# Weights and constants behind the first spreads, their low halves on GpSimd alone, and norm 1 behind the last maxima

## The reference, cut to what matters

```python
x = x + attention(layernorm(x), ctx, ctx, Wq, Wk, Wv, Wo)       # 16 batches of 256 tokens, width 256
x = x + ffn(layernorm(x), gate_w, w1, b1, w2, b2, sw1, sb1, sw2, sb2)
# attention: 16 heads of 16, softmax over pairs of 64-blocks (rows r, cols c, |r - c| <= band)
# ffn: out = shared(x) + sum over 2 experts e of relu(mask_e * x @ w1[e] + b1[e]) @ w2[e] + b2[e],
#      mask_e from the argmax of x @ gate_w.T; shared(x) = relu(x @ sw1 + sb1) @ sw2 + sb2
```

## Time and profile before

| | |
|---|---|
| median of 3 runs | 923.95 us (922.97 to 925.59) |
| the profiled execution, its own time | 924.62 us |
| its span | 922.8 us |
| PE busy | 798.9 us, 87% |
| DVE busy | 612.6 us, 66% |
| ACT busy | 498.0 us, 54% |
| POOL busy | 422.7 us, 46% |
| mean granted TensorE clock | 0.956 |

### The profile page before, as it was taken

One profiled execution on the slowest core, in us unless ns is written; L12 is line 12 of the kernel. 1 busy time (PEld: TensorE's weight loads), 2 busy tenths in 40 slices (PEclk: granted clock), 3 DMA queues, 4 the chain that ended last, 5 costly groups with the idle time before them and its releaser, 6 DMA issues.

```text
span 922.8 us, 24416 instructions
## 1 busy us (share of the span) xinstructions
PE 798.9 (87%) x8374; PEld 665.5 (72%) x8374; DVE 612.6 (66%) x1255; ACT 498.0 (54%) x1150; POOL 422.7 (46%) x773
## 2 busy tenths in 40 slices
PE   2165887879999999999999999999999999989894
PEld 2144756567887878687878787887878687858894
DVE  4558567476767677786858586767678685845231
ACT  2345453546565564757465656556574746465452
POOL 3455332343537373644546363637364554455311
PEclk9568899999999999999999999999999999999998
DMA  6767321263634444445445353434444444414630
GB/s 189 198 185 255 101 77 47 81 197 103 198 94 135 159 120 154 142 137 158 144 129 178 114 193 102 154 123 135 159 124 143 153 139 128 156 47 138 223 122 23
DMA packets 97389, 128.19 MB, mean 139 GB/s; under 512 B 14656, under 2 KB 82624, under 8 KB 97089
## 3 DMA queue, kind: packets, MB, share of 16 engines
q1 hardware_dynamic: 89760, 107.89, 37.9%
q0 software_dynamic: 6624, 18.95, 6.2%
q10 hardware_dynamic: 960, 0.79, 0.4%
HBM read 90.80 MB, written 37.04 MB: 139 GB/s over the span
## 4 chain that ended last, share of the span: by engine, by line
PE 49%; DVE 21%; DMA 13%; issue 6%; ACT 4%; SPq 4%; POOL 1%; DVEq 1%; POOLq 0%; ACTq 0%
PE acc L729 12%; PE nd L643 12%; PE hid L538 10%; DVE nmax L1186 9%; DMA QP<-scratch_m 5%; PE work L627 5%; DMA scratch_m<-mT 3%; PE work L671 2%; DVE xhat L1159 2%; PE work L538 2%; DVE PT L1229 2%; DVE T L1202 1%; PE work L594 1%; DVE check L1197 1%; SPq L341 1%
## 5 line engine op out<-in xcount | busy, mean ns | idle before, releaser
L1469 POOL TENSOR_TENSOR hl<-h,hh 128x256 fp32r<-128x256 f32 x228 | 172.3, 762 | 327.3 <-ACT hh L988 327.1
L972 ACT ACTIVATE PT<-work 128x512 f32<-128x512 f32 x192 | 106.1, 604 | 63.4 <-PE work L627 63.3
L1205 DVE RECIPROCAL T<-nd 128x256 f32<-128x256 f32 x51 | 89.4, 1753 | 42.9 <-PE nd L643 42.8
L729 PE MATMUL acc<-w_hi,hh 128*128 128x256 f32 (+1 forms) x528 | 113.6, 297 | 0.0
L538 PE MATMUL hid<-Xs,W 128*128 128x256 f32 x816 | 110.0, 288 | 0.2
L988 ACT ACTIVATE h<-hid,bias 128x256 f32<-128x256 f32 x144 | 69.1, 480 | 74.1 <-PE hid L538 74.1
L538 PEld LDWEIGHTS hid<-Xs,W 128*128 128x128 f32 x816 | 103.4, 195 | 2.7 <-DVE Xs L1139 0.9
L729 PE MATMUL acc<-w_lo,hh 128*128 128x256 f32 (+1 forms) x528 | 105.1, 281 | 0.0
L538 PE MATMUL hid<-Xr,W 128*128 128x256 f32 x768 | 104.1, 285 | 0.0
L538 PEld LDWEIGHTS hid<-Xr,W 128*128 128x128 f32 x768 | 94.2, 188 | 5.1
L643 PE MATMUL nd<-PT,V 128*32 128x256 f32 x1024 | 84.0, 400 | 10.1 <-DVE T L1202 4.5
(11 more groups left out here) (196 smaller groups left out, 1654.5 us busy)
## 6 DMA issues: line engine op xcount, KB each, us to landing
W<-w1q SPq DMA_DIRECT2D x64, 512.0 KB, 6.0
KP<-scratch_k SPq DMA_DIRECT2D x192, 64.0 KB, 2.4
QP<-scratch_q SPq DMA_DIRECT2D x180, 64.0 KB
scratch_k<-T SPq DMA_DIRECT2D x16, 512.0 KB, 3.5
scratch_q<-T SPq DMA_DIRECT2D x16, 512.0 KB, 3.2
yt<-yq SPq DMA_DIRECT2D x17, 260.0 KB, 2.8
xt<-xq SPq DMA_DIRECT2D x17, 256.0 KB, 3.8
xin<-x SPq DMA_DIRECT2D x16, 256.0 KB, 3.5
```

What stands on the lines that cost most here:

```text
L729: mm = nc.tensor.matmul(acc[:, t, :], R(h[:, u % 2, a, P * t:P * t + P]), R(row), start=first, stop=u == UNITS - 1 and h is hl and a == 1, ...
L972: nc.scalar.activation(PT[:, j % 4].rearrange("p t q -> p (t q)"), score_bank(j), ACT.Exp).then_inc(sem["exp_done"], 1)
L1205: nc.vector.reciprocal(T[:, p, :], nd[:, p % 2, 1, :]).then_inc(sem["inverted"], 1)
L1469: nc.gpsimd.tensor_tensor(R(hl[:, u % 2, a]), h32[:, u % 2, a], hh[:, u % 2, a], ALU.subtract).then_inc(sem["hl_done"], 1)
```

## The change

It has two parts.

In the start and in iteration 0: POOL's weight loads and SP's constants both wait for `q_spread1`, the second half of the spread Q. DVE no longer makes low halves of weights (it made every second one of the first 14); POOL makes all 24. They are handed out over iteration 0 by the table `SPLITS_AT`: 4 ahead of it, 2 and 2 around the projections of the next batch, one for each of the eight head pairs, then 3, and 5 at the very end. The sums of the constants on DVE (`make_constants`) move from ahead of the maxima to behind the Q projection of batch 1, with two temporary homes in `xhat2`, and PE's wait for them moves from `maxima` to the first `scores_t`. SP's first residual load moves behind them.

In all iterations from 1 on: DVE's `norm1_apply` moves from between the third and fourth group of maxima to behind the last; `gate_scores(n, 1)` and `choose` move from behind the second group to behind the third; `move_ids` moves to the head of the division loop; `ranks` on PE moves behind visit 3. On PE, ACT and DVE, K of the next batch stands ahead of `xT`.

```diff
-EARLY_PIECES = 4
-STAGES, BY_VECTOR = 5, 14
+STAGES = 5
+SPLITS_AT = (4, 0, 0, 0, 0, 2, 2, 1, 1, 1, 1, 1, 1, 1, 1, 3, 5)
...
         def slot_pieces(k):
-            return range(EARLY_PIECES + 2 * (k - 1), EARLY_PIECES + 2 * k)
+            return range(sum(SPLITS_AT[:k]), sum(SPLITS_AT[:k + 1]))
...
# SP
-            sp.wait_ge(sem["proj_lo"], 4)
+            sp.wait_ge(sem["q_spread1"], 96)
             for dst, src in ((bias1[:, :], b1), (bsum[:, :], blocksum), (hsum[:, :, :], headsum),
...
-            sp.wait_ge(sem["consts_read"], 1)
-            load_residual(0, first=True)
             iteration(0, False, False, True)
# PE
             def maxima(i):
-                if type(i) is int and i == 0:
-                    pe.wait_ge(sem["consts_read"], 1)
...
                 if p == 0:
                     pe.wait_ge(sem["shift_spread"], 32 * i + 32)
+                    if type(i) is int and i == 0:
+                        pe.wait_ge(sem["consts_read"], 1)
...
                     shared_up(n, 2)
-                    ranks(n, claim(i, ("rk", 0), tile=tile))
                 visit(i, 3, more)
                 if shared:
+                    ranks(n, claim(i, ("rk", 0), tile=tile))
                     shared_down(n, 1)
...
                 if more:
+                    front_project(i + 1, "k", 1, c_hi, c_lo, "c_lo")
                     front_xT(i + 1)
-                    front_project(i + 1, "k", 1, c_hi, c_lo, "c_lo")
# ACT, iteration
                 for p in range(PAIRS):
-                    if p == 2:
-                        splits(i, 7)
-                    if p == 5:
-                        splits(i, 8)
+                    splits(i, 7 + p)
...
-                splits(i, 9)
+                splits(i, 15)
...
-                splits(i, 10)
+                splits(i, 16)
# DVE, iteration
                     for j in range(4 * v, 4 * v + 4):
                         maximum(i, j)
-                        if shared and j == 13:
+                        if shared and j == 14:
                             rank_tokens(n)
-                    splits(i, v + 1)
...
-                    if shared and v == 1:
+                    if shared and v == 2:
                         gate_scores(n, 1)
-                        if type(i) is not int or i > 1:
-                            move_ids(n - 1)
                         choose(n)
-                    if shared and more and v == 2:
-                        norm1_apply(i + 1)
...
+                if shared and more:
+                    norm1_apply(i + 1)
                 low(i, "mT_hi", work[:, BANK[("mT", 0)], 0:P], mT[:, 0, :], mT[:, 1, :], "m_lo")
...
+                if type(i) is int and i == 0:
+                    make_constants()
                 for p in range(PAIRS):
                     if p == 0:
+                        if shared and (type(i) is not int or i > 1):
+                            move_ids(n - 1)
# POOL
-            pool.wait_ge(sem["first_q_bounced"], 16)
+            pool.wait_ge(sem["q_spread1"], 96)
             for n in range(STAGES):
                 load(n)
...
                 if more:
                     context_low(i + 1)
-                for k in range(3 if shared else 5, 10):
+                for k in range(5, 16):
                     splits(i, k)
...
                 reciprocal_deviation(i, 1)
-                splits(i, 10)
+                splits(i, 16)
```

More of the change, by code:

```diff
@@ L225, in loaded @@
             return sem[f"stage_loaded{SLOTS[n]}"], 16 * SLOTS[:n + 1].count(SLOTS[n])
[L227 to L230 removed]
         def low_done(n):
[L234 to L235 removed]
+            return sem["stage_lo"], n + 1
         def slot_pieces(k):
[L239 removed]
+            return range(sum(SPLITS_AT[:k]), sum(SPLITS_AT[:k + 1]))
         def low_half(g, a):
@@ L416, in iteration @@
                     load_x(i + 2)
-                if type(i) is not int or i > 0:
+                if type(i) is int and i == 0:
+                    sp.wait_ge(sem["consts_read"], 1)
+                    load_residual(0, first=True)
+                else:
                     load_residual(i)
```

71 lines of the change are left out of this document (21 added, 50 removed).

## The result

The changed kernel takes 914.65 us (median of 6 runs, 914.43 to 918.78) against 924.6 for the kernel before (6 runs): ratio 0.9907, 95% interval 0.9892 to 0.9921. The prediction was 914.4. The profiled execution spans 912.7 us instead of 922.8.

The account below looks back on a forecast made before the run. PE, busy 87% of the span, was taken as nearly the bound from iteration 4 on. Loop 5.3 us (6.4 + 1.2 - 2.3) plus start 4.3 (8.7 - 1 - 3.4) gave 9.6: 914.4 us, range 907 to 921.

Parts of the forecast that it names:

- the first wait: PE's 0.66 us ahead of visit 3's odd scores: becomes a wait for the mask at ranks, 0.1 comes back.
- the second: PE's 0.71 us wait ahead of the transposition of the maxima: goes, 0.7 gained per iteration.
- a gate score waits for c_lo: DVE, steady loop: one gate score stands until POOL's c_lo ends at 406.3, so the mask is there at 407.1.
- norm 1 is free: DVE, behind the last maxima: norm 1 takes 0.8 with POOL idle and costs nothing; without that cover 0.4.
- my 0.8: Gain per steady iteration, 0.1 + 0.7 from the two waits; over eight iterations 6.4 us.
- the price of the gate's move: Iterations 1 to 4: gate scores of about 1.5 replace a norm of 1.2; losses 0.3, 0.1, 0.5, 0.4.
- Iterations 1 to 4 gain nothing from the norm: Norm 1's move wins nothing there: iteration 4 transposes without a wait, in 1 to 3 maxima are late for other reasons.
- that chain: Start: from POOL's c_lo at 41.4 through K, xT, Q and constant sums, 10.1 us; transposed scores at 51.5, 8.7 earlier.
- The tail: End of iteration 0: five POOL splits behind norm 2's deviation delay visit 1 of iteration 1; 3.4 us lost, at least 2.7.
- nothing blocks the gate scores: Rival, steady loop: gate scores meet no POOL instruction; loop gains 12.4, start 4.3, 907.3 us; chance 0.13.
- The late pieces behind the store: Rival, iteration 1: last pieces land late, PE waits 8 us, start gives nothing back; 918.7 us; chance 0.17.
- The rival in which the mask holds PE longer in every iteration: At ranks behind visit 3: mask at 408.3, PE goes on 1.1 later; 930.6 us; chance 0.07.

Follow-up runs that it names:

- experiment 2: The changed kernel with the order of the loop put back as before, only the new start kept: 921.4 us, ratio 0.9963.
- experiment 10: The changed kernel with xT ahead of K again in all engines: 913.1 us, ratio 0.9864.
- Experiment 3: The changed kernel with gate scores, mask and ranks at their old places, norm 1 still behind the last maxima: 910.3 us, ratio 0.9857.
- experiment 5: The changed kernel with the store to w1q held until all 24 weight pieces have their low halves: 913.9 us, ratio 0.9871.
- experiment 4: The changed kernel with POOL making c_lo behind the third hidden unit's low halves from iteration 1 on: 907.1 us, ratio 0.9809.
- experiments 5 to 10: The changed kernel with store later (913.9 us), even splits (917.7), both (915.5), context first (913.3), constants first as well (913.0), or xT first (913.1).
- 6: The changed kernel with two of the five last weight pieces made inside iteration 0's division loop: 917.7 us, ratio 0.9900.
- 8: The changed kernel with the context of batch 1 split ahead of the first four weight pieces: 913.3 us, ratio 0.9862.
- experiment 9: The changed kernel with batch 1's context split ahead of the first four weight pieces and constant sums ahead of Q's low half: 913.0 us, ratio 0.9874.
- experiment 12: The changed kernel with later c_lo, gate scores, mask and ranks at old places in iterations 1 to 3, and context and constants first: 894.5 us, ratio 0.9674.

## Why the prediction was right, and where it was not

**The steady loop.** Predicted 7.6 from iteration 5 on (6.4 + 1.2), measured 8.3. The steps are as described: the first wait changes its name, the second goes, a gate score waits for c_lo, norm 1 is free. The eight iterations with both waits gained 1.03 each on average, 8.3 in all for 6.4, and iteration 15 gained 1.0 for 0.6. Against that, iteration 5 lost 1.2 where I had a gain of 0.3 (50.3 for 49.1). PE waits in iteration 4's division loop, between the two transpositions, which the kernel before did not do:

```profile
275.86 0.64 PE L638 MATMUL nd<-PT,V 128*32 128x256 f32 x8 [1.19 <-DVE T L1197]
```

DVE is late there because it waits 5.07 for the DMA of `scratch_q`, 3.54 before. A wait at this place (0.54 to 1.33) stands in all experiments but 2, so it comes with the new loop; why that DMA ends later is open. The 0.2 that each of the eight gained beyond my 0.8 is as large as a wait that I had not counted (0.21 to 0.45 for `scratch_m` ahead of the transposed scores before, at most 0.20 after). But with xT first (experiment 10) waits of up to 0.48 are back there and the iterations are not longer for it, so the cause of the 0.2 is not shown.

**Iterations 1 to 4.** Predicted -2.3, measured -0.8 in the profiled execution, but by other terms. What failed is the price of the gate's move: 1.3 (0.3, 0.1, 0.5 and 0.4 in iterations 1 to 4). Experiment 3 measures 5.0 for it, of which 3.9 are idle time of PE: the mask alone is waited for 0.32, 1.12, 1.11 and 1.31. In iteration 4, where I had 0.4, DVE is held by two instructions of POOL and not one. "Iterations 1 to 4 gain nothing from the norm" is off as well, by an amount that is not settled. With norm 1 (and K) moved and the gate left, they take 165.7 instead of 169.9. PE's idle time is 24.6 for 25.7 there, so of the 4.2 only 1.1 is waiting, and the rest is busy time, 141.1 for 144.2, at a granted clock of 0.97 for 0.94. Busy time differs by 3.4 between the kernel before and experiment 2, which have the same loop. The two errors nearly cancel; that is luck.

**The start.** Predicted 4.3, measured 2.6. The transposed scores came at 52.4 for 51.5. The two waits in that chain, 1.50 for a_lo and 2.43 for the constant sums, were in my sum (1.4, and 1.3 + 1.1); the 0.9 is many small sizes: K starts 0.4 later than I had it, Q 0.2 later behind K, and the scores 0.3 later behind Q. The division loop lost 1.9 and not 1 (21.2 before, 23.1 now), at the upper end of its 0 to 2. The tail cost 3.4 as predicted (11.2 to 14.55 from attention's output to visit 1), for the reason given, POOL's five splits; the late loads beside the store lay under it, as experiment 5 shows. Also, this execution was 0.8 ahead of that of before at 15 us, where the kernels don't yet differ, so the start's own gain is nearer 2. The runs give the start alone 3.4 (1.9 to 4.8).

**The sum** hit, 914.4 for 914.65, partly by luck: it was 0.7 too low from iteration 5 on, 1.5 too low in iterations 1 to 4 and 1.7 too high in the start. The steps named for the start and the steady iterations are what the traces show, and the sizes are off by up to 2 us in each part.

**The rivals.** That nothing blocks the gate scores was worth 907.3 by the prediction; made true, it is 907.1, though from iteration 5 on it gained 18.0 where that price had 12.4, and in the profiled execution the start and iterations 1 to 4 together lost 0.7 (91.6 and 171.6) where it had a gain of 4.3; the agreement is in part chance. The late pieces behind the store happened and were covered. The rival in which the mask holds PE longer in every iteration did not come: in iterations 5 to 14 the wait is 0.61 to 0.71. But what it described, a gate score and then the mask held by two instructions of POOL, is what iteration 4 shows, with a wait of 1.31. Where c_lo was moved onto the mask, in iterations 2 and 3 of experiment 4, the wait is 2.05 and 2.04.

**What stays open.** Why iterations 1 to 4 take 171 us in the changed kernel and 174 to 178 in experiments 5 to 10, whose order is the same there but for xT and K in one. It is mostly busy time at a lower clock (142.2 us busy in the changed kernel, 144.9 to 149.5 in these). Each was profiled once, and the runs of one kernel among them differ by up to 6.7 us; in 5, 6, 8 and 10 the profiled execution was the slowest of its kernel, in 9 the fastest. That a late gate costs 3 to 4 us of waiting in iterations 1 to 4 is shown by the idle times. That it also costs clock is argued: experiment 9 has half clock behind the mask's waits of iterations 2 and 3, the changed kernel has 0.66 behind that of iteration 2 (155 to 160 us) and a whole clock behind that of iteration 3.

## What to carry to other kernels

When an instruction is long in one place and short in another, look at the start and end of the other engine's instructions around it: a move of one POOL instruction by about 4 us, with no work saved, was worth 0.9 per iteration, about as much as the whole reordering of DVE's and PE's own work (0.95). A change that is one edit in the text may be several in time: the gate's move and norm 1's move acted in different iterations with different signs, and only one of them was good. And time won in a start can be given back in the iterations behind it; compare where a fixed point of each iteration stands, and not only the end. Split what is lost there into idle time and busy time: here the idle time told the edits apart, and the busy time of one execution did not.

## What the runs showed of the hardware

- A DVE instruction of 0.16 us took 1.09 and ended 0.01 behind the POOL instruction beside it (experiment 4, iteration 2); the gate score of 0.41 took 1.38 beside c_lo and ended 0.29 behind it (changed kernel, iteration 7). With POOL idle both had their short times (experiment 4, iteration 7).
- Three weight loads of 256 KB took 8.6, 7.8 and 7.2 us from issue to copy beside the store to `w1q`, and 3.8, 3.1 and 3.1 without it (changed kernel and experiment 5).
- TensorE's granted clock was 1.00 from 145 to 150 us, 0.52 in the next 5 us, and 0.50 again from 205 to 210 in experiment 9, each time right behind waits of 0.60 and 1.1. In the changed kernel it was 0.66 behind the same waits in iteration 2 (155 to 160) and stayed at 1.00 behind those in iteration 3 (205 to 215). In the steady loop it was 1.00 throughout (360 to 750 us), with two waits of 0.7 near the end of an iteration (kernel before), with one (changed kernel) and with none (experiment 12).
